# Rounding weights on two engines by chunk, and the last tile's FFN pieces and output chain dealt anew

## The reference

```
x: 1 x 2048 x 512, f32; 16 heads of 32; chunks of 16 tokens
h = layernorm(x)
q = silu(h Wq); k = h Wk, normalised per head; v = h Wv; beta = 2 sigmoid(h Wbeta)
for each chunk of 16 tokens, per head, with a state S (32 x 32):
    kh = k S;  v_new = gradient of a layernorm loss of kh against (v - k)
    A = tril(q k^T) * beta
    qh = q S - A v_new;  o = q + LN(qh, ln_w, ln_b)
    S = S - (k * beta)^T v_new
og = o * sigmoid(h Wg1 Wg2);  og = og * rsqrt(mean(og^2)) per head, * norm_w
x = x + layernorm(og Wo)
g = silu(layernorm(x) round8(gate_w) * gate_s);  u = (... round8(up_w)) * up_s
x = x + layernorm(((g * u) round8(down_w)) * down_s)          I = 1536
```

## Time and profile before

| | |
|---|---|
| median of 3 runs | 873.86 us (873.23 to 876.57) |
| profiled execution | 873.76 us, of which the span of instructions is 872.0 |
| busy over the span | PE 783.4 (90%), DVE 676.3 (78%), ACT 498.4 (57%), POOL 481.3 (55%) |
| mean granted clock of TensorE | 0.963 |
| chain that ended last | PE 62%, DVE 17%, POOL 9%, ACT 6%, issue 4% |

### The profile page before, as it was taken

One profiled execution on the slowest core, in us unless ns is written; L12 is line 12 of the kernel. 1 busy time (PEld: TensorE's weight loads), 2 busy tenths in 40 slices (PEclk: granted clock), 3 DMA queues, 4 the chain that ended last, 5 costly groups with the idle time before them and its releaser, 6 DMA issues.

```text
span 872.0 us, 24457 instructions
## 1 busy us (share of the span) xinstructions
PE 783.4 (90%) x9068; PEld 594.6 (68%) x9068; DVE 676.3 (78%) x2704; ACT 498.4 (57%) x1328; POOL 481.3 (55%) x848
## 2 busy tenths in 40 slices
PE   8877777688978999999999999999999999978896
PEld 5655444476756777777768687776777777766695
DVE  3778887887878788878887888778887888868444
ACT  2776674767657565664657466656565565623331
POOL 5455746665555665646564656565565656545300
PEclk9998998888989999999999999999999999989998
DMA  8012120211201001000100010000100010001000
GB/s 278 26 50 61 37 63 25 74 38 29 65 30 38 15 2 50 2 26 2 50 2 27 2 39 14 26 2 2 50 2 26 2 50 2 2 2 49 1 25 25
DMA packets 16728, 28.58 MB, mean 33 GB/s; under 512 B 3521, under 2 KB 3521, under 8 KB 16609
## 3 DMA queue, kind: packets, MB, share of 16 engines
q1 hardware_dynamic: 16608, 27.02, 9.9%
HBM read 22.82 MB, written 4.19 MB: 31 GB/s over the span
## 4 chain that ended last, share of the span: by engine, by line
PE 62%; DVE 17%; POOL 9%; ACT 6%; issue 4%; SPq 1%; DMA 0%; POOLq 0%; DVEq 0%; ACTq 0%
PE bank L638 20%; PE bank L426 10%; PE bank L671 8%; PE bank L614 5%; PE bank L589 4%; POOL rho L1205 3%; PE bank L575 3%; PE bank L566 3%; PE bank L440 3%; PE bank L476 2%; DVE work L1517 2%; PE bank L460 2%; PE bank L597 2%; ACT BDq L953 2%; PE bank L454 1%
## 5 line engine op out<-in xcount | busy, mean ns | idle before, releaser
L1205 POOL TENSOR_TENSOR rho<-sy,cst 128x2 f32<-128x2 f32 x128 | 89.7, 701 | 221.6 <-DVE sy L1490 221.6
L589 PEld LDWEIGHTS bank<-VX,BDkR 128*64 128x64 f32 x1024 | 44.7, 138 | 81.6 <-issue 34.9
L589 PE MATMUL bank<-VX,BDkR 128*64 128x64 f32 x1024 | 56.2, 230 | 36.7 <-DVE VX L1526 36.0
L1533 DVE TENSOR_TENSOR SQ<-SQ,bank 128x128 f32<-128x128 f32 x128 | 36.5, 285 | 65.5 <-PE bank L589 64.6
L970 ACT ACTIVATE qhR<-bank 128x64 f32<-128x64 f32 x128 | 28.6, 223 | 101.5 <-PE bank L597 100.9
L929 ACT ACTIVATE BDkR<-kR,cst 128x128 f32<-128x128 f32 x256 | 81.6, 401 | 0.0
L671 PE MATMUL bank<-DW,fh 128*128 128x512 f32 x188 | 78.7, 419 | 0.6 <-DVE fl L1606 0.6
L915 ACT ACTIVATE BDk<-bank 32x256 f32<-32x256 f32 x124 | 46.5, 375 | 54.1 <-DVE kR L1432 45.8
L671 PE MATMUL bank<-DW,fl 128*128 128x512 f32 x188 | 74.6, 397 | 0.0
L566 PEld LDWEIGHTS bank<-SQ,BDk 128*64 128x64 f32 x1024 | 46.2, 140 | 40.7 <-issue 38.5
L1512 DVE SCALAR_TENSOR_TENSOR work<-work,rho,rR 128x32 f32<-128x32 f32 x256 | 53.1, 249 | 26.5 <-POOL rho L1205 26.3
(11 more groups left out here) (170 smaller groups left out, 2167.8 us busy)
## 6 DMA issues: line engine op xcount, KB each, us to landing
xt<-in_x SPq DMA_DIRECT2D x16, 256.0 KB, 2.9
x<-in_x SPq DMA_DIRECT2D x16, 256.0 KB, 3.0
out<-x SPq DMA_DIRECT2D x16, 256.0 KB, 2.1
yb<-in_gate_w SPq DMA_DIRECT2D x12, 256.0 KB, 2.7
yb<-in_up_w SPq DMA_DIRECT2D x12, 256.0 KB, 2.7
yb<-in_down_w SPq DMA_DIRECT2D x12, 256.0 KB, 2.7
Wk<-in_wk SPq DMA_DIRECT2D x1, 1024.0 KB, 6.7
Wv<-in_wv SPq DMA_DIRECT2D x1, 1024.0 KB, 8.4
```

What stands on the lines that cost most here:

```text
L589: ins = mm(dS[p, e], bdkr[:, gh, j % 4, p], VX[:, e], start=True, stop=True, skip_group_check=True)
L1205: tt(dst, src, cst[:, C_NH:C_NH + n], ALU.pow).then_inc(*one)
```

## The change

It has two parts.

Rounding: `by_scalar(u)` holds for chunks worked on in steps 1 to 5, and in step 6 where t + 1 is 1 to 3. For these there is no `exponent` on VectorE; ScalarE does an Abs of the weights with scale 2^20 - 4 (which has the same exponent as before, with the mantissa kept), then Relu with scale 1 and Identity. `from_weight` stands at the place in ScalarE's step given in the diff, `from_exponent` where `magic` stood. `sized` gives the semaphore that Relu waits for.

Last tile: the pieces of tile 15 are put at other steps, the down piece of (6,0) and g of (6,2) come into it from the drain, (6,0)'s `fl` goes to VectorE. Its output chain is done in two halves, steps 0 to 3 and 4 to 7 (`end_...`, with buffers of their own), of which the first reaches its root `rq` in step 6; its product with Wo goes into bank PA[0] and waits for no residual. VectorE, ScalarE and GpSimd have a new order in the drain.

```diff
-            return c % 3 == 2 or c > NR * (LAST - 1)
+            return c % 3 == 2 or c >= NR * (LAST - 1)
...
+        def by_scalar(u):
+            t, j = next((t, j) for t in range(NT) for j in range(NC) if u in unit_before(t, j))
+            return j in (1, 2, 3, 4, 5) or (j == 6 and early(t + 1))
...
             def post_wo(n):
-                pe.wait_ge(post_v.sem, post_v.at("ogT", n))
+                bank, src = PA[1], ogT
+                if n == NT - 1:
+                    pe.wait_ge(*end_v.at("T", 1))
+                    bank, src = PA[0], ogL
...
-                else:
-                    if begun(n - 1):
-                        pe.wait_ge(tail_v.sem, tail_v.at("x1", n - 1))
+                elif n + 1 < NT:
+                    pe.wait_ge(tail_v.sem, tail_v.at("x1", n - 1))
...
@@ PE, drain @@
-                    down(p - 1, 0)
-                    for r in (2, 3):
-                        up(p - 1, r)
-                        down(p - 1, r - 1)
+                    ffn_u(p - 1, 2, 0)
+                    ffn_u(p - 1, 2, 1)
+                    down(p - 1, 1)
+                    up(p - 1, 3)
+                    down(p - 1, 2)
                     post_wo(n)
@@ PE, body, before write_state @@
+                    if j == 3 and t == NT - 1:
+                        ffn_down(*ffn[0], 0)
+                        ffn_down(*ffn[0], 1)
+                        ffn_g(*ffn[1])
...
+                    if j == 4 and t == NT - 1:
+                        ffn_g(*ffn[2])
+                    if j == 5 and t == NT - 1:
+                        ffn_u(*ffn[2], 0)
+                        ffn_u(*ffn[2], 1)
+                    if j == 6 and t == NT - 1:
+                        ffn_down(*ffn[1], 0)
+                        ffn_down(*ffn[1], 1)
+                        ffn_g(LAST - 1, 2)
...
@@ PE, body, after write_state @@
                     if j == 3 and 1 in ffn:
+                        if t == NT - 1:
+                            ffn_u(*ffn[1], 0)
                         ffn_u(*ffn[1], 1)
@@ ScalarE @@
+            def end_qsq(i):
+                act.wait_ge(scan_a.sem, scan_a.at("qh", NC * (NT - 1) + 4 * i + 3))
...
+                fn(four(sqL, i), four(qhR[(NT - 1) % 2], i), ACT.Square).then_inc(*end_a.one("qsq"))
...
+            def from_weight(t, j):
+                for u in unit_before(t, j):
+                    if by_scalar(u):
+                        act.wait_ge(s_stage[u % 2], 16 * (u // 2 + 1))
+                        if u:
+                            act.wait_ge(s_quant, u)
...
+                        fn(wmg[:, :], wst[u % 2][:, :], ACT.Abs, scale=STEEP).then_inc(s_size, 1)
+                        magic(u, 1.0)
...
@@ ScalarE, drain @@
+                    end_qsq(1)
+                    ffn_silu(p - 1, 2)
+                    end_osq(0)
                     fin_yc(2 * (p - 2) + 1, 1)
-                    post_qsq(n, n % 2)
-                    ffn_fh(p - 1, 1)
-                    ffn_silu(p - 1, 2)
+                    end_osq(1)
+                    ffn_fh(p - 1, 2)
                     tail_xc(n - 1)
-                    post_osq(n)
-                    ffn_fh(p - 1, 2)
                     ffn_silu(p - 1, 3)
@@ GpSimd, drain @@
-                    post_rq(n)
+                    end_rq(1)
+                    end_ro(0)
+                    end_ro(1)
                     tail_ra(n - 1)
-                    post_ro(n)
@@ VectorE @@
             def exponent(u):
+                if by_scalar(u):
+                    return
...
+            def end_og(i):
+                s = (NT - 1) % 2
+                dve.wait_ge(*end_g.at("rq", i))
+                tt(four(oL, i), four(qhR[s], i), wide_four(rqL, i), ALU.mult).then_inc(*end_v.one("n"))
...
+                tt(four(oL, i), four(oL, i), wK[:, :].rearrange("p (gh e) -> p gh e", gh=2).unsqueeze(2)
+                   .broadcast_to([P, 2, 4, DH]), ALU.mult).then_inc(*end_v.one("w"))
...
+                tt(four(oL, i), four(oL, i), four(qR[s], i), ALU.add).then_inc(*end_v.one("o"))
...
+                stt(out=four(oL, i), in0=four(thR[s], i), scalar=1.0, in1=four(oL, i), op0=ALU.add, op1=ALU.mult)\
+                    .then_inc(*end_v.one("og"))
...
@@ VectorE, drain @@
-                    tail_stats(n - 1)
-                    post_qss(n)
-                    ffn_fl(p - 1, 1)
-                    fin_out(p - 2, 1)
-                    post_n(n, n % 2)
-                    last_nw_product(n)
-                    post_o(n, n % 2)
-                    post_og(n, n % 2)
-                    ffn_f(p - 1, 2)
-                    post_oss(n)
-                    ffn_fl(p - 1, 2)
-                    tail_x1(n - 1)
-                    ffn_f(p - 1, 3)
-                    post_on(n)
-                    post_ogT(n)
-                    ffn_fl(p - 1, 3)
+                    ffn_fl(p - 1, 1)
+                    end_qss(1)
+                    end_og(0)
+                    end_oss(0)
+                    end_og(1)
+                    ffn_f(p - 1, 2)
+                    end_oss(1)
+                    end_ogT(0)
+                    ffn_fl(p - 1, 2)
+                    end_ogT(1)
+                    tail_stats(n - 1)
+                    fin_out(p - 2, 1)
+                    ffn_f(p - 1, 3)
+                    ffn_fl(p - 1, 3)
+                    tail_x1(n - 1)
                     tail_stats(n)
...
```

More of the change, by code:

```diff
@@ L212, in build @@
         post_g = Steps(sem("post_g"), "qse rq nw ose ro")
-        last_post, last_nw = Steps(sem("last_post"), "qse rq ose ro"), sem("last_nw")
+        end_v = Each(sem, "end_v", "qss n w o og oss on T")
+        end_a, end_g = Each(sem, "end_a", "qsq osq"), Each(sem, "end_g", "qse rq ose ro")
         tail_t = Steps(sem("tail_t"), "wo")
@@ L333, in unit_before, with sized, four, eight @@
             return unit_at(t, j - 1)
-        def post_roots(n):
-            return (last_post, 0) if n == NT - 1 else (post_g, n)
+        def by_scalar(u):
+            t, j = next((t, j) for t in range(NT) for j in range(NC) if u in unit_before(t, j))
+            return j in (1, 2, 3, 4, 5) or (j == 6 and early(t + 1))
+        def sized(u):
+            n = sum(by_scalar(m) == by_scalar(u) for m in range(u + 1))
+            return (s_size if by_scalar(u) else s_exp), n
+        sqL, oL, ogL = kn, xnT, xn
+        qssL, rqL, ossL, roL = kss, rk, qss, rq
+        def four(t, i):
+            return t[:, :].rearrange("p (gh j e) -> p gh j e", gh=2, e=DH)[:, :, 4 * i:4 * i + 4]
+        def eight(t, i):
+            return t[:, 8 * i:8 * i + 8].rearrange("p (gh j) -> p gh j", gh=2)
+        def wide_four(t, i):
+            return eight(t, i).unsqueeze(3).broadcast_to([P, 2, 4, DH])
         def own(h):
@@ L981, in post_osq, with end_osq @@
                 fn(o1[:, :], o2[:, :], ACT.Square).then_inc(*post_a.one("osq"))
+            def end_qsq(i):
+                act.wait_ge(scan_a.sem, scan_a.at("qh", NC * (NT - 1) + 4 * i + 3))
+                if i == 0:
+                    act.wait_ge(*prep_v.at("thR", NT - 1))
+                fn(four(sqL, i), four(qhR[(NT - 1) % 2], i), ACT.Square).then_inc(*end_a.one("qsq"))
+            def end_osq(i):
+                act.wait_ge(*end_v.at("og", i))
+                fn(four(sqL, i), four(oL, i), ACT.Square).then_inc(*end_a.one("osq"))
             def tail_xc(n):
@@ L1247, in post_rq, with end_root, end_rq, end_ro @@
                 pool.wait_ge(post_v.sem, post_v.at("qss", n))
-                g, m = post_roots(n)
-                root(rq[:, :], qss[:, :], 1, g, "qse", "rq", m)
+                root(rq[:, :], qss[:, :], 1, post_g, "qse", "rq", n)
             def post_ro(n):
                 pool.wait_ge(post_v.sem, post_v.at("oss", n))
-                g, m = post_roots(n)
-                root(ro[:, :], oss[:, :], 2, g, "ose", "ro", m)
+                root(ro[:, :], oss[:, :], 2, post_g, "ose", "ro", n)
+            def end_root(dst, src, eps, add_name, name, i):
+                e = slice(8 * i, 8 * i + 8)
+                tt(src[:, e], src[:, e], epses[:, eps:eps + 1].broadcast_to([P, 8]), ALU.add).then_inc(*end_g.one(add_name))
+                pool.wait_ge(*end_g.at(add_name, i))
+                power(dst[:, e], src[:, e], 8, end_g.one(name))
+            def end_rq(i):
+                pool.wait_ge(*end_v.at("qss", i))
+                end_root(rqL, qssL, 1, "qse", "rq", i)
+            def end_ro(i):
+                pool.wait_ge(*end_v.at("oss", i))
+                end_root(roL, ossL, 2, "ose", "ro", i)
             def tail_ra(n):
@@ L1743, in body @@
                         prep_rR(t + 1, o)
+                    if j == 7 and t == NT - 1:
+                        ffn_f(*ffn[2])
                     if scan:
```

119 lines of the change are left out of this document (79 added, 40 removed).

## The result

| | before | after |
|---|---|---|
| median | 873.86 us | 867.11 us (866.94 to 869.05) |
| ratio of the two | | 0.991, 95% interval 0.989 to 0.993 |
| profiled execution, span | 873.76, 872.0 | 868.21, 866.4 |
| mean granted clock | 0.963 | 0.968 |

The changed kernel is 6.75 us faster by the medians and 7.7 by the ratio (interval 6.2 to 9.3); the two terms of the forecast make 7.7. The page of after: busy time, then the chain that ended last.

What follows compares the result with a forecast made beforehand. PE bounds steady tiles; room lay in the rounding tiles, whose waits mostly run through VectorE, and in the last tile with its drain. 873.76 - 5.3 (rounding) - 2.4 (drain -3.2, tile +0.8) = 866.0 us, own range 861.5 to 869.5.

Steps and rivals of the forecast that it cites:

- Rounding, 5.3: Tiles 0 to 4: statistics 0.52 us earlier where PE idles for VX, 6.9 gained less 0.7 and 0.9, 5.3 us gained.
- Step 5 of tiles 3 and 4: After it PE waits for ScalarE's qhR copy, so the 0.52 and 0.42 us gained there are handed back.
- the chunks of step 6 in tiles 1 and 2: Rounding steps in which moving the exponent to ScalarE was counted as gaining 0.52 and 0.35 us.
- step 2 of tile 4: A rounding step counted as gaining 0.45 us, as PE there idled less than 0.52 us for VX.
- Tables: ScalarE's activation tables: Abs is in every set and loads nothing; were it elsewhere, 50 switches would cost 133 us.
- The rival of 938 us: Abs loads tables on ScalarE: 50 loads of 1.28 us, 938 us in all; chance 0.01.
- Tile 15, +0.8: Last tile: moved pieces lengthen steps 3, 4 and 6 and shorten step 5 by 1.7; sum 0.8 us longer.
- Drain, -3.2: After the last VX: 3.7 us of pieces removed, idle 4.0 in place of 3.5, Wo at +12.0; 3.2 us shorter.
- Passes over halves: Output chain in half-width passes: 0.45 us each, bounds 0.35 and 0.474; skill's formula gives 0.42 for 256 columns.
- ScalarE takes VectorE's place: Rival, tiles 0 to 4: ScalarE's added passes cost 7.0 us with none of the gain, 878.4 us; chance 0.07.
- The step is PE's anyway: Rival: statistics move up but PE does not, and the last tile's stalls eat its gain, 870 to 874; chance 0.18.
- More comes through: Rival: nearly every step gives 0.5 (12 us), or the drain loses its stalls, 856 to 861 us; chance 0.15.

Runs made afterwards that it cites:

- round_only: The kernel before with the rounding change alone, last tile and drain as they were: 869.28 us, ratio 0.9925 (0.9909 to 0.9940).
- vector_kept: The changed kernel, but VectorE still does an unread pass of the exponent's size for each of the 25 chunks: 871.38 us, ratio 0.9960.
- abs_added: The kernel before with 25 unread Abs passes added on ScalarE, VectorE keeping its exponents: 875.44 us, ratio 0.9999 (0.9984 to 1.0014).
- after_again: The changed kernel as it is, measured a second time against the kernel before: 867.43 us, ratio 0.9909 (0.9890 to 0.9929).
- all_scalar: The changed kernel with all 36 chunks' exponents given to ScalarE in place of 25: 871.34 us, ratio 0.9956 (0.9941 to 0.9972).
- pieces_back: The changed kernel with down(6,0) and g(6,2) put back from the last tile to the head of the drain: 870.89 us, ratio 0.9955.
- tail_only: The changed kernel with no chunk given to ScalarE, last tile and drain as changed: 874.27 us, ratio 0.9979 (0.9966 to 0.9992).

## Why the prediction was right, and where it was not

The sum said 7.7 us; 6.75 came by the medians and 7.7 by the ratio. The median lies 1.1 over the forecast 866.0 and inside the range. The mechanism, VectorE's exponent leaving the path, held; that the sizes came out so close is in part luck, as errors cancelled in each of the three terms. Point by point:

- *Rounding, 5.3.* Measured 5.3 by families of traces (by round_only's ratio 6.6, interval 5.3 to 8.0). The cause is shown, for most of it, by vector_kept and abs_added. Where it is gained and lost was read wrongly. The count took idle time of PE alone, but idle time fell by only 2.1 us; 3.1 came as matmuls at a higher clock, which stood in no term. Step 5 of tiles 3 and 4, where PE's wait for qhR was to hand back 0.9, gained 0.5 each (6.7 to 6.3 and 6.8 to 6.3 by family means). The loss is 2.5 us, in steps 6 and 7 of tiles 0 to 2. There the prediction had 0.52 and 0.35 gained by the chunks of step 6 in tiles 1 and 2 and 0.62 lost by that of tile 0, a gain of 0.25. The step that failed is "GpSimd's shift of a chunk still waits for VX, now 0.5 earlier; Relu and Identity end about 0.5 before that". It was true of 13 shifts of 26 (before, 20 waited for VX). In sum the other steps gained 7.8, forecast 5.3 - 0.25 = 5.05, and these lost 2.5, forecast a gain of 0.25: two errors of 2.7 that cancelled.
- *One step did not gain what was counted.* In step 2 of tile 4 the prediction counted 0.45. In before, what set that step was not VX: fl on VectorE ran beside the shift on GpSimd, took 1.75 us, against 0.68 by itself, and held up the addition to the state. In after the shift comes late, behind ScalarE, and the two no longer overlap. The rows of before:

```profile
241.10 1.64 POOL L1293 TENSOR_TENSOR yb<-x,yb 128x512 f32<-128x512 f32 x1 [1.18 <-DVE VX L1526]
...
241.54 1.75 DVE L1606 TENSOR_TENSOR fl<-f,fh 128x512 fp32r<-128x512 f32 x1
```

and of after:

```profile
239.12 0.68 DVE L1704 TENSOR_TENSOR fl<-f,fh 128x512 fp32r<-128x512 f32 x1
...
239.83 1.27 POOL L1393 TENSOR_TENSOR yb<-x,yb 128x512 f32<-128x512 f32 x1 [2.35 <-ACT x L1077]
```

But PE now waits 2.13 us for ScalarE's qhR copy in front of its product with Wk, where it waited 0.13 in before, and so the step is hardly shorter: 8.14 us in after_again for 8.36, and 9.8 in after, where that product ran at a granted clock of 0.68 and took 5.33 us in place of 3.63. In after:

```profile
236.91 0.42 PE L601 MATMUL bank<-SQ,BDq 128*64 128x32 f32 x8 [2.13 <-ACT qhR L1016]
237.17 5.33 PE L452 MATMUL bank<-Wk,xnT 128*64 128x512 f32 x16
```

Steps 2 and 3 together are 1.1 us shorter by family means (16.3 to 15.2). How much of that is the overlap and how much the clock, no run separates.

- *Tables.* after has one ACT_TABLE_LOAD, 1.28 us at 0.73, and 25 Abs passes without another. The Trainium skill (ScalarE: Activation LUTs, "Table sets: the hidden batching unit") has abs in every set, and the trace agrees. The rival of 938 us is dead.
- *Tile 15, +0.8.* The three traces with the old order have 45.7 in the mean (44.9 to 46.6), those with all of the new one and no filling 46.3 (seven, 45.9 to 47.0): 0.7 for 0.8, the size of the scatter. The terms by step were further off. By the same means steps 3 and 4 grew by 2.4 us together (1.96 forecast), step 5 shrank by 2.8 (1.7), step 6 grew by 0.8 (0.5) and step 7 by 0.3 (nothing), so the close sum is luck in part. Part of what step 3 costs is its clock: with the idle time of steps 1 and 2 filled, the tile with two pieces more took 44.4. The old order had a slow step 3 too and was not run filled, so the two orders are not compared at a full clock.
- *Drain, -3.2.* From 77.4 to 74.0 where the clock held, so 3.3 (the term was right to 0.1), and to 75.6 where it didn't. Wo at +11.7, the waits 1.0 and 2.05 for 1.5 and 1.6. The xl of the last pair waits 0.56 in every trace, as in the kernel before, so the 0.6 counted for it was nothing new, and the 0.3 for down(6,2) did not occur; but the 0.63 in front of down(6,5), counted as removed, stayed. These cancel nearly. The step that failed is the one that priced the silu's hold at its length alone: it costs 2.05 of waiting and, in three of six traces, 1.5 to 1.6 of clock.
- *Passes over halves.* 0.418 us each. The formula of the Trainium skill (VectorE: DVE Perf Modes, "The TRN2 errata — SBUF-src ops pay a fixed extra latency per instruction") gives 0.42 for 256 columns, as an estimate, and the trace agrees. Its advice to make tiles of 512 elements and more did not decide here, where PE's FFN work covered the small ones: Wo came 5.5 us sooner after VX.
- *Rivals.* "ScalarE takes VectorE's place" decides for the three chunks of step 6 and for the eleven that all_scalar adds. For the other 22 it has a part only: PE's waits for the qhR copy grew by 3.7 us in tiles 0 to 4. "The step is PE's anyway" did not come true for tiles 0 to 4: they gained the 5.3, and more would have come. In the last tile and the drain the moved pieces are what paid. "More comes through" was there to be had: with the two misplaced silus and the clock taken care of, 860.81.

## What to carry to other kernels

Ask of every wait that a new order leaves on PE not only how long it is, but what PE's granted clock does behind it; here waits of 1.8 to 3.0 us were followed, where the clock fell, by 1.5 to 1.7 us lost in slow matmuls. A pass moved off the engine on the path gains its length only where nobody then waits for the engine that takes it: go through the steps one by one, and leave the operation where it was in those where the receiver has a backlog that a third engine waits for. Judge a part by families of traces and by undoing it, since one trace against another was 2 us off here.

## What the runs showed of the hardware that was not expected

- The same work around a wait of 2.01 to 2.05 us (1.77 in pieces_back) is followed by 1.2 GHz in three traces (after, after_again, pieces_back) and not in three others (tail_only, vector_kept, all_scalar). The stretch from 2.5 us before the end of that wait to 11.5 behind it has a granted clock of 0.88 in after and 1.00 in tail_only. What decides it is open; the runs only show that it goes away with the wait.
- Ten matmuls of no use, put into the idle time ahead of a step, made it 1.5 us shorter, the clock of that step rising from 0.75 to 1.00.
- Two passes over 128x512 with two operands each, one on VectorE and one on GpSimd, took 1.75 and 1.64 us where they overlapped, and 0.68 and 1.27 where they did not. The one on VectorE started second and ended 0.55 us behind the other.
- Abs with an immediate scale is 0.10 us shorter than Relu with a bias column over the same 128x512 (0.617 against 0.72).
- The power on GpSimd costs 0.70 over 2 columns, 1.64 and 1.83 over 8 and 2.90 over 16.
